# Perceiver block on one core: attention scores in 32 by 32 tiles of the array over four PSUM banks, the q projection and the scaling of probabilities at step 1

## The chip, the cores and the metric

The program runs on one core of a Trainium2 chip. The metric is the device time of one execution in microseconds; before the change three executions took 1400.08, 1402.43 and 1406.96 us (median 1402.43).

## What is computed

x is (32, 32, 512), that is 32 batches of 32 rows; ctx is (32, 257, 512). Three parts follow one another, each with a layer norm ahead and x added behind:

```python
x = x + xattn(layernorm(x), ctx, ctx, mask, Wq, bq, Wk, bk, Wv, bv, Wo, bo)   # 16 heads of 32, softmax over 257
x = x + attn(layernorm(x), Wqkv, bqkv, Wout, bout, gamma, beta)               # causal linear attention, elu + 1
x = x + ffn(layernorm(x), gate_w, shared_*, expert_*)                         # 64 experts, top 8 by sigmoid, I = 256
# in xattn, for each batch:
scores = einsum('bnlh,bnph->bnlp', q, k) / sqrt(32)   # 16 heads, 32 x 257 each
out    = einsum('bnlp,bnph->bnlh', softmax(where(mask, scores, -1e8)), v) @ Wo.T + bo
```

## The kernel before

Two stages follow one another on the core. `stage_a` (lines 96 to 1018) computes both attentions, the shared part of the experts for the first four row tiles and the routing; `stage_b` (from line 1049) loads the experts' weights and computes them for gathered rows. The change touches `stage_a` alone. What follows is about it.

The 1024 rows of x make 8 tiles of 128 rows, of 4 batches each. Every engine has its own instruction queue, in which it goes through the same walk (`body`, line 206): for each tile t, for each of its batches b, six steps k = 0 to 5; the step's number in the tile is s = 6 b + k. The engines meet through semaphores. Tiles 0 and 1, the last tile and a closing pass are written out, the tiles between are a loop (`passes`, line 221). A queue is served strictly in order, so what stands ahead of an instruction on its engine holds it up even where its data are ready.

For batch n = 4 t + b, TensorE does (`per_batch`, line 833): at k = 0 to 3 one fourth of the keys each (12 matmuls, into banks 0 and 1 in turn), at k = 4 and 5 half of the values each (12 matmuls of 512 columns, banks 0 and 1). Keys and values are computed as three products of rounded parts (`ch` high, `cl` low). The softmax of a batch is finished while the next one is projected ("carried"): the scores of batch n are computed in steps 4 and 5, two groups of four heads each (line 891). For that ScalarE writes q of the batch into `qb`, a matrix of 128 x 128 for each group whose blocks off the diagonal are zero (`q_blocks`, line 428), so one matmul over all 128 rows gives four heads. The two score banks (2 and 3) serve the four groups in turn, and VectorE clips each by the mask into `prob` (line 638), then takes the maximum (641) and the bias of the exponential (643). ScalarE exponentiates two groups at step 0 and two at step 1 of the next batch (`exps`, line 443); VectorE scales by the reciprocal of the sum at step 2 (`scaled`, lines 586 to 595). At step 4 TensorE transposes the probabilities in two halves through one bank (`prob_t`, line 827; the bank is `at_ps`, number 4) which ScalarE copies to `att` (line 472), and at step 5 multiplies them by the values into `av_ps`, bank 5 (lines 878, 879). VectorE adds the last position's value and writes `ot` (`attended`, line 597).

Two lists place other work in these steps. `PRE` prepares the next tile: the layer norm of x at step 4 ("norm": VectorE, with a root on GpSimd, line 369, for which VectorE waits), its transposes at step 18 ("xT", line 803), its q projection at step 20 ("q", `pre_q`, lines 809 and 557). `POST` (line 67) finishes the tile before: output projection at step 6 ("oproj", line 933), transposes of the normed x at 9, q, k, v of the linear attention at 10 and 11 (lines 941, 945), its products at 14 to 17 (lines 954, 964), "outproj" at 19 (line 968) whose result goes through two norms on VectorE (lines 696 to 706), the transposes of the third norm's result at 22 ("x3T", line 936) and the router (line 971) with a chain of short operations on VectorE (707 to 733), and "pos" at 23, after which VectorE computes the slot indices (744) and GpSimd scatters eight columns of entries (line 407). GpSimd's root for the next "norm" stands behind these scatters. In the closing pass the rest of the last batch and tile is done, with the shared experts between (`SHARED`, line 70).

## Time and profile before

| | us |
|---|---|
| median of three runs | 1402.43 |
| the profiled execution | 1397.42 |
| its span, first to last instruction | 1395.7 |
| TensorE busy | 1302.3 (93%) |
| VectorE busy | 780.5 (56%) |
| ScalarE busy | 628.1 (45%) |
| GpSimd busy | 395.6 (28%) |
| mean granted TensorE clock | 0.979 |

All rows come from the one profiled execution. Times are microseconds from the start of its span. PE is TensorE, DVE VectorE, ACT ScalarE, POOL GpSimd, SP SyncE; Lnnn is a line of the kernel. A matmul in float32 shows as two records. Its duration includes the way through the array, so records overlap and the distance between two starts is what each costs TensorE in a row. What stands in square brackets is the idle time of the engine just before, with what ended it.

### The profile page before, as it was taken

What the parts mean: (1) busy time and instruction counts of PE and PEld (TensorE: products, weight loads), DVE (VectorE), ACT (ScalarE), POOL (GpSimd) and SP (SyncE); (2) the same over time, 40 slices, a digit from 0 to 9 for tenths busy, and PEclk for the clock granted to TensorE, in tenths of its full rate; (3) what the DMA queues carried; (4) which work ended last, traced back from release to release, by engine and by line L of the source; (5) the groups of instructions that cost most, each with busy time, mean ns of one, the idle gap of its engine ahead of it and who ended that gap; (6) DMA issues with size and microseconds to landing.
All of it is one profiled execution on the core that took longest, in us unless ns stands there. A gap on an engine that the chain in (4) does not pass through costs nothing. (4 is left out here: it accounts for less than half of the span.)

```text
span 1395.7 us, 28249 instructions
## 1 busy us (share of the span) xinstructions
PE 1302.3 (93%) x7526; PEld 1006.9 (72%) x7527; DVE 780.5 (56%) x1758; ACT 628.1 (45%) x1312; POOL 395.6 (28%) x314
## 2 busy tenths in 40 slices
PE   5999999999999999999997878999999999999991
PEld 4888878888887878788885534676676766667660
DVE  4445665665655656656565454656655565655540
ACT  3453444353443434443432105566656565665550
POOL 0002020030020200300301113356655556856531
PEclk9999999999999999999999989999999999999996
DMA  6722110201110101101003006799999999999884
GB/s 202 285 89 44 32 48 17 63 17 40 39 32 31 47 16 46 32 16 55 25 1 121 16 32 242 247 317 327 343 300 299 270 333 311 367 291 311 261 217 84
DMA packets 67186, 204.74 MB, mean 147 GB/s; under 512 B 16047, under 2 KB 18351, under 8 KB 56768
## 3 DMA queue, kind: packets, MB, share of 16 engines
q1 hardware_dynamic: 43248, 159.71, 31.6%
q0 software_dynamic: 23888, 44.40, 15.2%
q8 instruction: 27, 0.44, 0.1%
q14 instruction: 23, 0.19, 0.0%
HBM read 177.26 MB, written 37.03 MB: 154 GB/s over the span
## 5 line engine op out<-in xcount | busy, mean ns | idle before, releaser
L369 POOL TENSOR_TENSOR rstd<-vep,half 128x1 f32<-128x1 f32 x32 | 17.8, 556 | 576.4 <-DVE vep L532 576.3
L457 ACT ACTIVATE kt<-bank,colb 128x256 f32<-128x256 f32 x128 | 60.6, 474 | 243.4 <-PE bank L848 243.4
L846 PE MATMUL bank<-ch,wkh 128*128 128x256 f32 x512 | 158.6, 310 | 7.5 <-DVE cl L543 7.5
L1490 PE MATMUL ebank<-guh,xth 128*128 128x512 f32 x380 | 155.0, 408 | 1.6 <-DVE xtl L1383 0.8
L1378 DVE TENSOR_TENSOR gul<-wgu,guh 128x2048 fp32r<-128x2048 f32 x54 | 123.8, 2293 | 54.2 <-ACT guh L1295 54.2
L1225 POOL DMA_INDIRECT xg<-xn_rows,ig x95 | 126.9, 1336 | 87.9 <-issue 72.9
L1492 PE MATMUL ebank<-guh,xtl 128*128 128x512 f32 x380 | 149.1, 392 | 0.0
L1491 PE MATMUL ebank<-gul,xth 128*128 128x512 f32 x380 | 148.3, 390 | 0.0
L848 PE MATMUL bank<-ch,wkl 128*128 128x256 f32 x512 | 144.6, 282 | 0.0
L847 PE MATMUL bank<-cl,wkh 128*128 128x256 f32 x512 | 144.5, 282 | 0.0
L1520 PE MATMUL ebank<-wd,ht 128*128 128x512 f32 x292 | 134.3, 593 | 0.8 <-ACT ht L1280 0.8
L846 PEld LDWEIGHTS bank<-ch,wkh 128*128 128x128 f32 x512 | 97.6, 191 | 16.0 <-issue 14.3
L1295 ACT CAST guh<-wgu 128x2048 fp32r<-128x2048 f32 x54 | 102.9, 1906 | 7.5 <-DMA wgu<-in_egu 7.4
L862 PE MATMUL bank<-wvh,ch 128*128 128x512 f32 x256 | 105.6, 413 | 0.0
L407 POOL DMA_INDIRECT slot_table<-entry,idx x61 | 59.9, 981 | 153.3 <-DVE idx L744 137.1
L1285 ACT ACTIVATE sg<-ebank 128x256 f32<-128x256 f32 x95 | 36.5, 385 | 145.4 <-PE ebank L1492 135.5
L847 PEld LDWEIGHTS bank<-cl,wkh 128*128 128x128 f32 x512 | 97.7, 191 | 5.3 <-issue 5.0
L864 PE MATMUL bank<-wvh,cl 128*128 128x512 f32 x256 | 101.3, 396 | 0.0
L863 PE MATMUL bank<-wvl,ch 128*128 128x512 f32 x256 | 100.9, 394 | 0.0
L848 PEld LDWEIGHTS bank<-ch,wkl 128*128 128x128 f32 x512 | 97.4, 190 | 0.0
L1373 DVE TENSOR_TENSOR h<-ebank,sg 128x256 f32<-128x256 f32 x95 | 40.0, 424 | 86.3 <-ACT sg L1285 84.9
L1520 PEld LDWEIGHTS ebank<-wd,ht 128*128 128x128 f32 x292 | 51.4, 190 | 45.2 <-issue 44.0
(244 smaller groups left out, 2774.6 us busy)
## 6 DMA issues: line engine op xcount, KB each, us to landing
wgu<-in_egu SPq DMA_DIRECT2D x54, 1024.0 KB, 8.5
wd<-in_edn SPq DMA_DIRECT2D x54, 512.0 KB, 6.2
sgu<-in_egu SPq DMA_DIRECT2D x17, 1024.0 KB
craw<-in_ctx SPq DMA_DIRECT2D x32, 514.0 KB, 3.2
sdn<-in_edn SPq DMA_DIRECT2D x17, 512.0 KB, 5.3
wqkv<-in_wqkv SPq DMA_DIRECT2D x1, 3072.0 KB, 18.5
second_sums<-x1b SPq DMA_DIRECT2D x9, 256.0 KB, 3.7
xa<-in_x SPq DMA_DIRECT2D x8, 256.0 KB, 2.8
```

Of the source, the lines that this page charges most:

```text
L846: mm(out, wkh[:, c, w], h[:, c, :], start=c == 0, stop=False)
L847: mm(out, wkh[:, c, w], lo[:, c, :], start=False, stop=False)
L848: last = mm(out, wkl[:, c, w], h[:, c, :], start=False, stop=c == DC - 1)
L862: mm(out, h[:, c, r], wvh[:, c, :], start=c == 0, stop=False)
L864: last = mm(out, lo[:, c, r], wvh[:, c, :], start=False, stop=c == DC - 1)
L1225: nc.gpsimd.indirect_dma_start(tile.xg[item.q][:, :], None, d.xn, bass.IndirectOffsetOnAxis(ig[item.q][:, tile.half:tile.half + 1], 0), bo ...
L1295: nc.scalar.copy(guh[par][:, :, :], wgu[w][:, :, :]).then_inc(s_w["gu_high"], 1)
L1378: V.tensor_tensor(gul[par][:, :, :], wgu[w][:, :, :], guh[par][:, :, :].bitcast(F32), ALU.subtract).then_inc(s_w["gu_low"], 1)
L1490: mm(out, ah[:, c, :], bh[:, c, :], start=c == 0, stop=False)
L1491: mm(out, ah[:, c, :], bl[:, c, :], start=False, stop=False)
L1492: return mm(out, al[:, c, :], bh[:, c, :], start=False, stop=c == n - 1)
L1520: last = mm(y_ps[tile.half][:, :], tile.ht[:, c, :], wd[item.w][:, c, :], start=c == 0, stop=c == IC - 1)
```

## The change

- The four heads groups' scores are computed by 16 narrow matmuls a batch: for column group g and row group i, 32 rows of `qt` by 32 columns against the same 32 rows of the keys, straight from `qt`, into rows 32 g of bank i. The zero-padded `qb`, its copies on ScalarE and its clearing on GpSimd go.
- The score banks are now four: 2, 3, 5 and 0. Bank 0 is also that of the keys' first fourth, so keys at step 0 wait for the minimum that reads it, which VectorE takes first. Transposes and attended values share bank 4.
- On TensorE the scores are all at step 5, behind the second half of the transposes, which moves there from step 4; attended values come after the scores. They read `att` with a stride, as the heads now stand in another order. The four minima are all at step 5 on VectorE, ahead of `attended`. ScalarE's copy of the second half moves to step 5, ahead of the copy of the values.
- The q projection of the next tile moves from step 20 of the tile before to step 1 of its own tile. SyncE's load of x moves from step 20 to step 18.
- Scaling moves from step 2 to step 1 on VectorE.
- On ScalarE three more tiles of the loop are written out, on VectorE one; on TensorE none.
- Buffers of the shared experts' rows that lay in `qb` become two of their own.

The diff, cut to its core:

```diff
@@ -74,7 +74,8 @@
 PER = [sum(1 for n in STEPS if BANK[n] == b) for b in (0, 1)]
-PRE = {4: "norm", 18: "xT", 20: "q"}
+PRE = {4: "norm", 18: "xT"}
+PREQ = 1
@@ -104,7 +105,7 @@
         bank = [ctx.enter_context(nc.psum_tensor(f"bank{i}", [P, 512], F32)) for i in range(8)]
-        kv_ps, sc_ps, at_ps, av_ps, px = bank[0:2], bank[2:4], bank[4], bank[5], bank[6:8]
+        kv_ps, sc_ps, at_ps, av_ps, px = bank[0:2], (bank[2], bank[3], bank[5], bank[0]), bank[4], bank[4], bank[6:8]
...
@@ -211,6 +213,8 @@
                         on_pre(PRE[s], t + 1)
+                    if front and prev and s == PREQ:
+                        on_pre("q", t)
                     if prev:
@@ -218,12 +222,15 @@
-        def passes(eng, per_batch, on_post, on_pre, on_shared=None):
+        def passes(eng, per_batch, on_post, on_pre, on_shared=None, written_out=0):
...
             body(True, True, 1, True, per_batch, on_post, on_pre)
-            with eng.Fori(2, NT - 1) as t:
+            for t in range(2, 2 + written_out):
                 body(True, True, t, True, per_batch, on_post, on_pre)
+            if 2 + written_out < NT - 1:
+                with eng.Fori(2 + written_out, NT - 1) as t:
+                    body(True, True, t, True, per_batch, on_post, on_pre)
             body(True, True, NT - 1, False, per_batch, on_post, on_pre)
@@ -285,7 +292,7 @@
             def on_pre(n, t):
-                if n == "q":
+                if n == "xT":
...
@@ -425,20 +430,9 @@
-            def q_blocks(t, b):
-
-                n = BT * t + b
-                wait(act, s_pqe, t + 1)
-                wait(act, s_sc, 4 * n - 4)
-                for i in range(HG):
-                    r = slice(i * HD, (i + 1) * HD)
-                    last = nc.scalar.copy(qb[b % 2][r, :, i * HD:(i + 1) * HD], qt[r, :, b * L:(b + 1) * L])
-                last.then_inc(s_qb, 1)
-
             act.wait_ge(s_pt, 1)
...
             high(0, 0)
-            act.wait_ge(s_pad, 4)
@@ -453,27 +447,27 @@
                     wait(act, s_kv, 6 * n + k + 1)
-                    wait(act, s_sc, 4 * n)
+                    wait(act, s_sc, n)
                     nc.scalar.activation(kt[:, k, 0:S1], kv_ps[k % 2][:, 0:S1], ACT.Identity, bias=colb[:, 1, k:k + 1]).then_inc(s_ke, 1)
...
                 if k == 3 and front:
-                    if b == 0 and type(t) is int and t == 0:
-                        q_blocks(0, 0)
-                    if b < 3:
-                        q_blocks(t, b + 1)
                     if b < 3 or nxt:
...
                 if k == 4 and carried:
-                    for j in range(2):
-                        wait(act, s_tr, 2 * (n - 1) + j + 1)
-                        nc.scalar.copy(att[:, j, :], at_ps[:, :]).then_inc(s_at, 1)
+                    attention(n, 0)
+                    if not front:
+                        attention(n, 1)
+                if k == 5 and carried and front:
+                    attention(n, 1)
                 if k == 5 and front:
                     values(n, b, k)
-                if k == 5 and front and b == 3 and nxt:
-                    q_blocks(t + 1, 0)
+
+            def attention(n, j):
+                wait(act, s_tr, 2 * (n - 1) + j + 1)
+                nc.scalar.copy(att[:, j, :], at_ps[:, :]).then_inc(s_at, 1)
@@ -512,7 +506,7 @@
-            passes(act, per_batch, on_post, on_pre, on_shared)
+            passes(act, per_batch, on_post, on_pre, on_shared, written_out=3)
@@ -615,7 +609,7 @@
                     masks(t, b + 1) if b < 3 else masks(t + 1, 0)
-                if k == 2 and carried:
+                if k == 1 and carried:
                     scaled(t, b)
@@ -627,15 +621,13 @@
                         negate_last(t, b + 2) if b < 2 else negate_last(t + 1, b - 2)
+                if k == 5 and front:
+                    wait(dve, s_tr, 2 * (n - 1))
+                    wait(dve, s_sc, n + 1)
+                    for i in (HG - 1, *range(HG - 1)):
+                        V.tensor_tensor(prob[b % 2][:, i, :], sc_ps[i][:, 0:S], cap[b % 2][:, :], ALU.min).then_inc(s_sa, 1)
                 if k == 5 and carried:
                     attended(t, b)
-                if k >= 4 and front:
-                    for g in (2 * (k - 4), 2 * (k - 4) + 1):
-
-                        wait(dve, s_sc, 4 * n + g + 1)
-                        if g == 0:
-                            wait(dve, s_tr, 2 * (n - 1))
-                        V.tensor_tensor(prob[b % 2][:, g, :], sc_ps[g % 2][:, 0:S], cap[b % 2][:, :], ALU.min).then_inc(s_sa, 1)
                 if k == 5 and front:
...
@@ -757,7 +748,7 @@
             dve.wait_ge(s_pads, 16 * (NT + 1))
-            passes(dve, per_batch, on_post, on_pre, on_shared)
+            passes(dve, per_batch, on_post, on_pre, on_shared, written_out=1)
             dve.wait_ge(s_px[0], NT * PER[0] + 1)
@@ -840,6 +831,8 @@
                     wait(pe, s_ve, 2 * n - 1 + k) if k < 2 else wait(pe, s_ke, 4 * n + k - 1)
+                    if k == 0:
+                        wait(pe, s_sa, 4 * n - 3)
                     out = kv_ps[k % 2][:, 0:S1]
@@ -865,32 +858,34 @@
                     wait(pe, s_pn, n)
+                    wait(pe, s_od, n - 1)
                     prob_t(n, b, 0)
...
                         prob_t(n, b, 1)
+                if k == 5 and carried and front:
+                    prob_t(n, b, 1)
+                if k == 5 and front:
+                    wait(pe, s_ke, 4 * n + 4)
+                    wait(pe, s_ve, 2 * n + 1)
+                    wait(pe, s_sa, 4 * n)
+                    wait(pe, s_pqe, t + 1)
+                    wait(pe, s_pte, t + 2 if b == 3 and nxt else t + 1)
+                    pe.sem_inc(tick, 1)
+                    for g in range(DC):
+                        for i in range(HG):
+                            r = slice(i * HD, (i + 1) * HD)
+                            last = mm(sc_ps[i][g * L:(g + 1) * L, 0:S], qt[r, g, b * L:(b + 1) * L], kt[r, g, :], start=True, stop=True)
+                    last.then_inc(s_sc, 1)
                 if k == 5 and carried:
...
                     wait(pe, s_ve, 2 * n)
-                    wait(pe, s_od, n - 1)
                     pb = (b - 1) % 2
...
                         w = slice(g * P, (g + 1) * P)
-                        mm(av_ps[:, w], vb[pb][:, 0, w], att[:, 0, w], start=True, stop=False)
-                        last = mm(av_ps[:, w], vb[pb][:, 1, w], att[:, 1, w], start=False, stop=True)
+                        for j in range(2):
+                            heads = att[:, j, :].rearrange("p (i g n) -> p g i n", i=HG, g=DC)[:, g]
+                            last = mm(av_ps[:, w], vb[pb][:, j, w], heads, start=j == 0, stop=j == 1)
                     last.then_inc(s_av, 1)
-                if k >= 4 and front:
-                    if k == 4:
-                        wait(pe, s_qb, n + 1)
-                    for g in (2 * (k - 4), 2 * (k - 4) + 1):
-                        wait(pe, s_ke, 4 * n + g + 1)
-                        wait(pe, s_sa, 4 * n + g - 1)
-                        if g == 0:
-                            wait(pe, s_pte, t + 2 if b == 3 and nxt else t + 1)
-                        if g == 1:
-                            wait(pe, s_pqe, t + 2 if b == 3 and nxt else t + 1)
-                        mm(sc_ps[g % 2][:, 0:S], qb[b % 2][:, g, :], kt[:, g, :], start=True, stop=True).then_inc(s_sc, 1)
-                if k == 4 and carried and front:
-                    prob_t(n, b, 1)
                 if k == 5 and b == 0 and type(t) is int and t == 0:
@@ -900,6 +895,7 @@
                 if n == "q":
+                    wait(pe, s_sa, 4 * BT * t)
                     pre_q(t)
             def on_post(n, t):
```

## Rows read from the trace of the kernel before

**Rows 1.** Busy time by stage: tile 4, expert stage; the first line names columns.
```profile
core 0: us, PE busy (x) PEld busy (x) DVE busy (x) ACT busy (x) POOL busy (x), PEclk, DMA share, GB/s
...
376.40:471.70 95.30, 92.65 (x659) 78.50 (x658) 58.25 (x141) 37.91 (x102) 12.58 (x14) 1.00 0.11 35
...
840.40:1395.70 555.30, 518.93 (x2172) 355.64 (x2172) 299.10 (x593) 317.76 (x481) 293.10 (x194) 0.97 0.92 283
```

**Rows 2.** SyncE's issues in order of time, around the end of the attention stage (start, length).
```profile
840.36 0.33 SPq L1173 DMA_DIRECT2D wgu<-in_egu  x1
```

**Rows 3.** TensorE in order of time, tile 4's fourth batch: start, length, line, operation, tiles, records.
```profile
449.01 3.60 PE L968 MATMUL bank<-wout,xt 128*128 128x512 f32 x8
...
453.86 3.73 PE L813 MATMUL bank<-xat,wq 128*128 128x128 f32 x32
...
461.65 0.60 PE L830 MATMUL bank<-cn,prob 128*128 128x128 f32 x4
462.09 1.03 PE L891 MATMUL bank<-kt,qb 128*128 128x257 f32 x4
462.98 0.66 PE L830 MATMUL bank<-cn,prob 128*128 128x128 f32 x4
463.47 0.60 PE L936 MATMUL bank<-cn,xn 128*128 128x128 f32 x4
464.88 1.10 PE L971 MATMUL bank<-gate,xt 128*128 128x64 f32 x8 [0.80 <-ACT xt L494]
```

**Rows 4.** VectorE in order of time, same batch and the next tile's first.
```profile
459.48 0.55 DVE L534 TENSOR_SCALAR xn<-x,mv,rstd 128x512 f32<-128x512 f32 x1 [0.76 <-POOL rstd L369]
...
460.19 1.14 DVE L594 TENSOR_SCALAR prob<-prob,rr 128x257 f32<-128x257 f32 x4
...
476.30 0.17 DVE L744 CAST idx<-a 128x8 int32<-128x8 f32 x1
...
488.01 1.51 DVE L534 TENSOR_SCALAR xa<-xa,mv,rstd 128x512 f32<-128x512 f32 x1 [3.25 <-POOL rstd L369]
489.44 1.18 DVE L608 TENSOR_TENSOR ot<-bank,vlc 32x128 f32<-32x128 f32 x4
490.65 0.76 DVE L638 TENSOR_TENSOR prob<-bank,cap 128x257 f32<-128x257 f32 x2
```

**Rows 5.** ScalarE in order of time, same two batches.
```profile
463.67 0.59 ACT L472 COPY att<-bank 128x512 f32<-128x512 f32 x1 [0.75 <-PE bank L830]
...
478.02 1.20 ACT L435 COPY qb<-qt 32x128 f32<-32x128 f32 x4
```

**Rows 6.** GpSimd in order of time, next tile's first batch.
```profile
487.39 0.58 POOL L369 TENSOR_TENSOR rstd<-vep,half 128x1 f32<-128x1 f32 x1
```

**Rows 7.** TensorE in order of time, end of that first batch.
```profile
487.05 1.03 PE L891 MATMUL bank<-kt,qb 128*128 128x257 f32 x4
...
490.75 3.69 PE L933 MATMUL bank<-wo,ot 128*128 128x512 f32 x8 [1.26 <-DVE ot L608]
```

**Rows 8.** TensorE in order of time, small tiles of the array in tile 4's linear attention.
```profile
429.17 1.16 PE L954 MATMUL bank<-raw,x 32*128 32x128 f32 x16
...
437.99 1.08 PE L964 MATMUL bank<-am,cn 128*32 128x128 f32 x32
```

**Rows 9.** TensorE in order of time, tile 7's fourth batch and behind it.
```profile
744.98 1.12 PE L830 MATMUL bank<-cn,prob 128*128 128x128 f32 x4 [2.88 <-DVE prob L594]
...
748.19 0.60 PE L936 MATMUL bank<-cn,xn 128*128 128x128 f32 x4
...
757.43 1.06 PE L986 MATMUL bank<-cn,craw 128*128 128x128 f32 x8 [0.90 <-DVE prob L638]
760.59 5.37 PE L995 MATMUL bank<-sgu,wq 128*128 128x512 f32 x8 [2.10 <-ACT wq L507]
```

**Rows 10.** Busy time of two stretches, same columns as group 1.
```profile
744.00:747.00 3.00, 2.02 (x7) 1.83 (x8) 0.94 (x5) 0.59 (x1) 0.00 (x0) 0.58 0.84 266
762.00:765.00 3.00, 3.00 (x5) 1.10 (x4) 1.55 (x5) 0.00 (x0) 2.39 (x3) 0.51 0.98 369
```

More of the change, by code:

```diff
@@ L133, in stage_a @@
         vlc = sb("vlc", [P, DC, NB])
-        qb = [sb(f"qb{i}", [P, DC, P]) for i in range(2)]
+        rows = [sb(f"rows{i}", [P, D]) for i in range(2)]
         prob = d.prob
@@ L162, in stage_a @@
         idx, entry = d.idx, d.entry
-        flat = [a[:, :, :].rearrange("p c s -> p (c s)") for a in (craw[0], craw[1], qb[0], qt, qb[1], xat)]
+        flat = [a[:, :, :].rearrange("p c s -> p (c s)") for a in (craw[0], craw[1], qt, xat)]
+        flat = flat[0:2] + [rows[0][:, :], flat[2], rows[1][:, :], flat[3]]
         sx, sy = [a[:, 0:D] for a in flat[:4]], [a[:, D:2 * D] for a in flat[:2]] + flat[4:]
@@ L167, in stage_a @@
         sht = [wq[:, 3, j * I:(j + 1) * I].rearrange("p (c n) -> p c n", c=IC) for j in range(2)]
-        sd_ps = [at_ps, av_ps]
+        sd_ps = [bank[4], bank[5]]
         s_sl = [sem(f"shared_rows_in{j}") for j in range(SHA)]
@@ L338, in _ @@
                 load_shared(j, sx[j], sy[j], s_sl[j])
-            sp.wait_ge(s_sc, 4 * NB)
+            sp.wait_ge(s_sc, NB)
             sp.wait_ge(s_pq, NT)
@@ L361, in _ @@
             nc.gpsimd.memset(pad[:, :, 1], 0.0).then_inc(s_pad, 1)
-            for i in range(2):
-                nc.gpsimd.memset(qb[i][:, :, :], 0.0).then_inc(s_pad, 1)
-            pool.wait_ge(s_pad, 4)
+            pool.wait_ge(s_pad, 2)
             def root(n):
@@ L649, in on_pre @@
                 if n == "q":
-                    wait(dve, s_qb, 4 * t)
                     pre_q(t)
```

2 lines of the change are left out of this document (1 added, 1 removed).

## The prediction

> **What bounds the kernel now.** I read the table of stages first. In a tile of the attention stage TensorE is busy 92.7 of 95.3 us, VectorE 58, ScalarE 38, GpSimd 13, the DMA engines 11% [rows 1]: the stage runs at TensorE's pace. The expert stage begins at 840 us with DMA at 0.92, and its first load of expert weights is issued at 840.36 [rows 1, 2], so what the attention stage saves arrives earlier one for one. Then TensorE's timeline over one tile's fourth batch [rows 3] shows where work leaves and which wait comes next; VectorE's rows [rows 4], ScalarE's [rows 5] and GpSimd's [rows 6] give the chains that run beside it; [rows 7] is the one regular wait of TensorE (1.26 us). Below, K is the start of a tile's first keys, O the end of its outproj issue. For tile 4, the next K is 471.7 (the stage table is cut there [rows 1]) and O = 449.01 + 3.03 = 452.05 (eight matmul records at 0.38).
>
> **Scores.** Now a half takes four records, 462.09 to 462.98, then the next transposes start: 0.89 us, so 1.78 a batch, 32 batches [rows 3]. After: 32 records of 257 columns, 32 rows by 32 columns of the array each. No row shows such a tile. The nearest ones: 16 records of 128 columns with 32 rows each, two row groups in turn, take 1.16 us, 0.073 a record; 32 records with 32 columns each, four column groups in turn, take 1.08 us, 0.034 [rows 8]; on the full array 32 such records take 3.73, 0.117 [rows 3]. So two and four tiles do overlap almost fully, along rows and along columns, and the four streams of the second case read all 128 rows. A record of 257 columns takes 0.22 alone. If all 16 tiles overlap, a batch is two rounds, 0.44, plus issue; if only four do, eight rounds, 1.78. Neither case of [rows 8] shows an issue limit of its own, since 0.034 is what four at a time give (0.117 / 4 = 0.029). For issue I take 0.2, for going into small tiles and back 0.25 (1.16 against 8 x 0.117 = 0.94): about 0.9. The upper bound, if 0.034 were an issue limit: 32 x 0.034 + 0.25 = 1.35.
>
> The Trainium skill (TensorE: Matmul & The Clock Gate, Part 3, measured speedup) gives 10.6 times for sixteen 32 x 32 tiles; my estimate from that page would be 16 x 0.44 / 10.6 = 0.66 us, inside the bounds above, for another data type.
>
> It hardly matters whether it is 0.7 or 0.9, because of a new order: the second transposes move from before to directly before the scores, and the attended matmuls then wait for their copy. A transpose group started at 462.98 has its copy from 463.67 to 464.26 [rows 3, 5], 1.28 after its start, 0.06 for the semaphore; it occupies TensorE 0.44, so 0.90 is left for the scores. Scores and this wait together: 0.9, a gain of 0.9 a batch. The clean-up that goes (four q copies on ScalarE, 1.20 us a batch [rows 5]) is off the path and costs or gives nothing directly; it lets the context's rounding and the xT copy come earlier. The strided read in the attended matmuls I put at nothing, as their column count stays at 128; bound 0 to 16 x 0.117 = 1.9 us a batch were it to halve the rate, for which no row speaks. Written-out loops on ScalarE and VectorE: nothing, bound plus or minus 2 us in all, since both have 40% and more idle [rows 1].
>
> **Fourth batch, O to the next K** (19.63 us). The q projection, 3.5 us, leaves it (3.73 with its tail [rows 3]), and so do the first half of the scores and the second transposes ahead of the third norm's transposes (x3T): 463.47 - 462.09 = 1.38. TensorE could then start x3T at 463.47 - 3.5 - 1.38 = 458.6. But x3T needs the norm chain on VectorE, which starts with outproj's result and ends at 459.48 + 0.55 = 460.03 [rows 4]; scaling at step 1 comes ahead of it, but its exps are over before outproj ends, so it doesn't delay it. **This is what is late next:** x3T at 460.1, a new wait of 1.5 us. From x3T to K are 8.2 us now (463.47 to 471.68); minus 0.89, plus transposes 0.44 and scores 0.9, gives 8.7. New length 8.05 + 8.7 = 16.8: gain 2.9. Had scaling stayed at step 2 the stall would be worse: its last multiply ends 1.3 us after the norm [rows 4], and the first transposes wait for it. Tile 7, which has no q projection, shows that stall: 2.88 us [rows 9].
>
> **First batch, K to oproj** (19.07). Scattering the slots holds GpSimd from the indices (476.30) to 487.39, and only then comes the root for the pre-norm; VectorE stands in its queue until the apply ends at 488.01 + 1.51 = 489.52, K + 17.8 [rows 4, 6]. The indices keep their distance from K (fewer scores, but all four minima now behind the router's chain: 0.2 earlier), so K + 17.65. Behind that apply stand the four minima (0.76 for two, so 1.52) and the addition of the values (1.18): 20.4, oproj at K + 20.5 [rows 4]. The change adds a wait here: the fourth score bank is the bank of the next keys, so keys of batch 1 wait for the first minimum, K + 18.1. TensorE comes there at 487.9 - 471.7 = 16.2 now (487.05 + 0.89 [rows 7]), plus 3.5 for q, minus 0.9: 18.8. So step 1 is where q pays: it covers this wait, with 0.7 to spare. Then keys, 20.2, and 0.3 of wait before oproj instead of 1.26 [rows 7]. K to oproj grows by 1.4. Tiles 1 and 7 have no root held up (tile 0 scatters nothing, tile 7 has no pre-norm), so there it grows by 3.5 - 0.9 = 2.6. Batches 1 and 2 lose 0.9 each. The earlier load of the next x rows on SyncE waits for the xT transposes; behind it stands one context load, landing long before its use.
>
> **Sum.** Tile 0: q 3.5 leaves it, 4 x 0.9: -7.1. Tile 1: -2.9 + 2.6 - 1.8 = -2.1. Tiles 2 to 6: 5 x (-2.9 + 1.4 - 1.8) = -16.5. Tile 7: its norm ended 1.3 before the first transposes at 744.98 (the scaling between [rows 4]), so x3T moves from 748.19 to 743.7 [rows 9], -4.5; behind it 8.2 becomes 8.7 as above, so -4.0; -4.0 + 2.6 - 1.8 = -3.2. Tail: the same order, 0. Together -28.9.
>
> **The clock.** A wait of 2.88 us was followed by a granted clock of 0.58 (most of the stretch at the 1.2 GHz level), and 0.90 idle, transposes, 2.10 idle by 0.51 [rows 9, 10], while 1.26 in every tile did not (1.00 [rows 1, 7]). The new 1.5, with short transposes and the 0.80 before the router [rows 3], lies between. A fall costs about 1.3 us of the values' matmuls; I take it in four of seven tiles: +5. Bounds 0 and +9. Total -24: from the profiled execution's 1397.4 (span 1395.7) to 1373. The median of the runs shown is 1402.4, 5.0 above it: 1378.
>
> **Rivals.** (1) Only four tiles overlap. Scores 1.78 + 0.25 = 2.03, so 1.1 x 32 = +35, of which the first batches' slack hides about 3: 1410. For it: nothing in [rows 8] goes beyond four. Against: rows and columns each give their full share. (2) Four overlap, and a weight load for a row group must wait until its running matmul is done: eight rounds of 0.22 + 0.11 (the load, put at the 0.117 pace of full records as a bound) + 0.25 = 2.9, so +2.0 x 32 = 64, less 3: 1439, slower. The whole change breaks even where scores take 0.9 + 24 / 32 + 3 / 32 = 1.75 a batch, which is 0.19 a round of eight, so both rivals are slower than before. Against: in the second case of [rows 8] all four tiles share the rows and still run at 0.034. The Trainium skill (same page, Part 3, the mechanism) says that weight loads overlap only where the row group differs, and this order returns to each row group after four matmuls; that rule speaks for (2), the trace against it. (3) The new bank wait: if the first minimum comes later than K + 18.8, each us late costs 1 us in five tiles; 3 to 4 us late adds 15 to 20: 1393 to 1398. Against: the margin is worked out, but only 0.7. (4) The change doesn't pack at all, 32 x 0.22 = 7 us a batch, 1570: the first case of [rows 8] excludes it nearly.
>
> **How the numbers follow.** Forecast 1378, chance 0.78, own range 1366 (no fall of the clock, -28.9, and some 7 us for the rest) to 1392 (scores at 1.35, +14). Rival 3: 0.06. Rival 1: 0.10. Rivals 2 and 4: 0.06. Range 1366 to 1397. A difference under 0.5% (7 us) can't be told from none. Faster by more: 0.78 + 0.03 = 0.81. Within: 0.03 and half of rival 1, 0.08. Slower: the other half and rivals 2 and 4, 0.11.
>
> **What would show it.** Scores: 32 records in 0.6 to 1.0 us a batch, attended matmuls waiting for ScalarE's copy. x3T waiting 1.3 to 1.7 us for VectorE's norm in each tile; K to K 92 in tiles 2 to 6; oproj's wait 0.6; q behind the second keys. Granted clock below 1.00 in some tiles. Wrong, if the scores take over 1.4 us, if keys wait for a minimum in the first batch, or if the expert stage doesn't move.

## The result and the profile after

| | before | after |
|---|---|---|
| median of four executions, us | 1404.70 | 1388.03 |
| lowest, highest | 1400.08, 1407.38 | 1386.48, 1388.64 |
| profiled execution, its span | 1397.42, 1395.7 | 1388.28, 1386.5 |
| mean granted clock of TensorE | 0.979 | 0.973 |
| records of TensorE's matmuls, of ScalarE | 7526, 1312 | 8294, 1184 |

The ratio after to before is 0.9883, 95% interval 0.9851 to 0.9915: faster by 1.2%. 1378 was forecast, with a range of 1366 to 1397. The medians differ by 16.7 us, the two profiled executions by 9.1, as the one of before ran below its four others; the lengths below are those of the profiles and account for the 9.1.

Busy time by stage, columns as in [rows 1]: tile 4, the closing pass and the rest of the changed kernel. The last two are cut at the start of TensorE's last group of down-projections of the shared experts, 821.6 us (828.5 in before). In this document that point is called the last K, and the time from it to the end the expert stage. The first matmul of `stage_b`, at which [rows 1] cut, comes later: at 840.4 in before and 832.2 in after, with 555.3 and 554.3 us to the end.

```profile
core 0: us, PE busy (x) PEld busy (x) DVE busy (x) ACT busy (x) POOL busy (x), PEclk, DMA share, GB/s
...
367.60:463.80 96.20, 90.91 (x755) 75.42 (x754) 58.18 (x141) 33.37 (x86) 12.72 (x14) 0.98 0.11 34
746.80:821.60 74.80, 56.17 (x295) 34.03 (x293) 35.60 (x76) 10.65 (x27) 11.94 (x13) 0.88 0.13 46
821.60:1386.00 564.40, 523.06 (x2183) 357.64 (x2182) 306.15 (x621) 317.83 (x481) 302.39 (x199) 0.97 0.91 280
```

TensorE gave back 1.7 us of busy time in tile 4, 92.65 to 90.91, and the tile still takes 96.2 us instead of 95.3 [rows 1]: its idle time doubled, from 2.65 to 5.29. Counted from one first key to the next, and from tile 7 on to the last K, the attention stage ends 6.9 us earlier and the expert stage is 2.3 us shorter, together 9.2 between the two spans. It splits so: tiles 0 and 1 -9.4 (forecast -9.2), tiles 2 to 6 +2.1 (forecast -16.5 before the clock), tile 7 -3.4 (forecast -3.2), closing pass +3.7 (forecast 0), expert stage -2.3, of which 1.2 lie ahead of the first matmul of `stage_b`. So what failed lies in tiles 2 to 6 and behind tile 7. The closing pass has two longer waits of TensorE: 3.25 us instead of 2.10 before the first of the shared experts' products, in e1 below too, and 3.37 instead of 1.37 for VectorE's addition to the last attended values, whose signal from TensorE came 2.0 us late in the way described next.

TensorE in order of time, tile 4's fourth batch, the answer to [rows 3]:

```profile
453.10 0.60 PE L821 MATMUL bank<-cn,prob 128*128 128x128 f32 x4
455.04 0.66 PE L932 MATMUL bank<-cn,xn 128*128 128x128 f32 x4 [1.34 <-DVE xn L528]
456.45 1.10 PE L967 MATMUL bank<-gate,xt 128*128 128x64 f32 x8 [0.75 <-ACT xt L488]
...
460.24 0.60 PE L821 MATMUL bank<-cn,prob 128*128 128x128 f32 x4
460.77 0.72 PE L877 MATMUL bank<-kt,qt 32*32 32x257 f32 x32
461.51 1.72 PE L887 MATMUL bank<-att,vb 128*128 128x128 f32 x13
```

This is the forecast order, row by row. The 32 records of the scores (L877) take 0.72 us; the third norm's transposes (L932) wait 1.34 for VectorE's norm (1.5 was forecast), the router 0.75; the attended matmuls (L887) start at 461.51. The row behind them is short of three records: 16 are issued. From outproj's end to the next K are 16.75 us (forecast 16.8).

The next batch, the same engine and then ScalarE and GpSimd, the answers to [rows 5 to 7]:

```profile
478.85 0.40 PE L857 MATMUL bank<-wvh,cl 128*128 128x512 f32 x1
482.20 0.74 PE L821 MATMUL bank<-cn,prob 128*128 128x128 f32 x4 [2.96 <-ACT att L470]
```

```profile
481.07 0.59 ACT L475 COPY vb<-bank 128x512 f32<-128x512 f32 x1 [5.20 <-remote]
481.56 0.59 ACT L470 COPY att<-bank 128x512 f32<-128x512 f32 x1
```

```profile
469.51 1.14 POOL L412 DMA_INDIRECT slot_table<-entry,idx  x1 [15.10 <-DVE idx L735]
...
478.80 0.96 POOL L412 DMA_INDIRECT slot_table<-entry,idx  x1 [0.30 <-issue]
479.77 0.58 POOL L374 TENSOR_TENSOR rstd<-vep,half 128x1 f32<-128x1 f32 x1
```

This was not foreseen. TensorE ended the first half of the values at 476.00 (its last record, L857, starts at 475.61 and takes 0.39), and ScalarE's copy of it started at 481.07. "Remote" means that the profile finds no instruction that ended the wait. The trace has the change of the semaphore that this record raises at 480.98: the signal came 5 us late, while GpSimd issued its scatters (K + 5.7 to K + 16.0). Four of TensorE's signals in this batch are over 1.4 us late, the first from K + 8.0. ScalarE's copy of the first transposes stands behind it in the queue, and TensorE waits 2.96 us for that. Tiles 2 to 7 show the same wait with 2.14, 2.60, 2.73, 2.96, 1.55 and 0.82 us. Behind them the clock is low:

```profile
482.20:488.40 6.20, 6.20 (x64) 4.94 (x64) 2.57 (x8) 1.07 (x2) 0.00 (x0) 0.72 0.00 0
```

K to oproj is 22.4, 24.4, 24.6, 24.7 and 21.9 us in tiles 2 to 6, where 20.5 was forecast. No signal of TensorE is over 0.7 us late in the attention stage in the profile of before, whose scatters stand at the same distance from K.

### The profile page after: what moved, and what is told of

Same layout as the page of the kernel before. It is cut to its first block and busy times, and to the rows that moved or that the text cites. A ratio compares the mean times of both kernels' runs of the same rounds, so it can differ in the third digit from the quotient of the medians.

```text
span 1386.5 us, 29315 instructions
## 1 busy us (share of the span) xinstructions
PE 1280.7 (92%) x8294; PEld 976.9 (70%) x8295; DVE 780.5 (56%) x1758; ACT 591.8 (43%) x1184; POOL 400.0 (29%) x312
## 5 line engine op out<-in xcount | busy, mean ns | idle before, releaser
L1374 DVE TENSOR_TENSOR gul<-wgu,guh 128x2048 fp32r<-128x2048 f32 x54 | 123.8, 2293 | 55.1 <-ACT guh L1291 45.8
L1221 POOL DMA_INDIRECT xg<-xn_rows,ig x95 | 130.2, 1371 | 82.7 <-issue 69.4
L857 PE MATMUL bank<-wvh,cl 128*128 128x512 f32 x256 | 102.1, 399 | 0.0
```

The source lines that it names most:

```text
L857: last = mm(out, lo[:, c, r], wvh[:, c, :], start=False, stop=c == DC - 1)
L1221: nc.gpsimd.indirect_dma_start(tile.xg[item.q][:, :], None, d.xn, bass.IndirectOffsetOnAxis(ig[item.q][:, tile.half:tile.half + 1], 0), bo ...
L1374: V.tensor_tensor(gul[par][:, :, :], wgu[w][:, :, :], guh[par][:, :, :].bitcast(F32), ALU.subtract).then_inc(s_w["gu_low"], 1)
```

## The experiments

The twelve kernels ran on four chips: e1 to e4 on one, e5 to e8 on a second, e9 to e11 on a third, e12 on a fourth, each time beside the kernel before (medians 1397.14, 1398.80, 1399.21 and 1397.35). Times are compared within a chip, lengths within the profiles. A table of them stands at the end of this section. A "fall" is a tile of 2 to 7 in which the length from outproj's end to K is over 1 us above the shortest of the kernel; in each of them the granted clock drops below 1.00.

**e1, the changed kernel again.** No edit.

> The changed kernel once more, unaltered. In its first profile TensorE's signal that half of the values is written reached ScalarE 2.6 to 5.1 us late in the first batch of tiles 2 to 6, and the step from K (first keys of a tile) to oproj took 21.9 to 24.7 us where 20.5 was forecast. Theory A (a property of the kernel): the same here, K to oproj 22 to 25 us, time 16 to 17 us under the kernel before. Theory C (a property of that one execution): K to oproj 20 to 21 us and a time about 25 us under before.

Measured: 1371.19 (1369.35 to 1372.91), ratio 0.9818 [0.9794, 0.9842], 26 us below before. K to oproj 20.2 to 20.6, outproj's end to K 16.75 in four of six tiles (the other two are falls), K to K 91.7 to 92.2 in tiles 3 to 6. The first batch of tile 5, on ScalarE and then on TensorE and VectorE:

```profile
466.69 0.59 ACT L475 COPY vb<-bank 128x512 f32<-128x512 f32 x1 [0.80 <-PE bank L857]
```

```profile
474.84 3.69 PE L929 MATMUL bank<-wo,ot 128*128 128x512 f32 x8 [0.44 <-DVE ot L602]
```

```profile
472.20 1.41 DVE L628 TENSOR_TENSOR prob<-bank,cap 128x257 f32<-128x257 f32 x4
```

The copy that came 5.20 us late now waits 0.80. With K at 454.2, the first minimum stands at K + 18.0 (forecast 18.1), the second keys start at 472.73, K + 18.5 (forecast 18.8), oproj at K + 20.6 (forecast 20.5) after a wait of 0.44 (forecast 0.3). So the late signals don't belong to the kernel alone, and where they are absent the steps of the prediction hold.

**e2, the scatters a tile later.** GpSimd issues them at step 7 of the tile after, which in a queue that works on tile t are those of tile t - 2. In short:

```
-    if n == "pos":           scatters of tile t
+    if 6 * b + k == 7:       scatters of tile t - 2
```

> The changed kernel with GpSimd's scatters of the slots moved from the end of a tile to step 7 of the tile after, behind oproj's work on GpSimd, where it has some 50 us to spare. Theory A, that the late signals come with the scatters and strike the first batch because they run there: K to oproj falls to 19.5 to 20.5 us in all tiles (the pre-norm's root is not held up either), five tiles gain 2 to 5 us and the time is 12 to 20 us under the changed kernel, unless the late signals only move along to steps 7 to 11, in which case the waits appear there and the gain is 0 to 8 us. Theory B (late signals from the written-out loops): K to oproj still 22 to 24 us, gain under 3 us.

Measured: 1381.14 (1375.37 to 1382.52), ratio 0.9892 [0.9871, 0.9913], 10 us slower than e1, where theory A had 12 to 20 under the changed kernel. This chip shows no late signals without the edit either (e1), so e2 can't tell whether they come with the scatters. K to oproj falls only from 20.2 to 20.6 to 20.0 to 20.2: TensorE's own work has that length. From outproj's end to K it is 16.8 to 20.4. Two stretches of e2, the same place of tiles 3 and 5 (columns as above), and then the rows of tile 6:

```profile
349.00:360.00 11.00, 8.89 (x34) 7.13 (x33) 7.43 (x24) 2.64 (x6) 0.55 (x1) 0.70 0.30 99
...
537.00:548.00 11.00, 8.86 (x82) 6.82 (x81) 8.30 (x27) 3.65 (x8) 0.55 (x1) 1.00 0.29 99
```

```profile
631.14 1.26 POOL L399 TENSOR_TENSOR xr<-xr,rowb 128x512 f32<-128x512 f32 x1
631.21 1.48 DVE L531 TENSOR_SCALAR xn<-x,mv,rstd 128x512 f32<-128x512 f32 x1 [0.76 <-POOL rstd L374]
632.74 0.66 PE L935 MATMUL bank<-cn,xn 128*128 128x128 f32 x4 [2.29 <-DVE xn L531]
```

Both stretches have the same x3T wait (1.35 and 1.36), and one is followed by a granted clock of 0.70, the other by 1.00. In tiles 6 and 7 a new cost comes on top: GpSimd's addition, which stood behind the scatters, now runs beside VectorE's norm, whose last step takes 1.48 instead of 0.55 us, and the wait grows to 2.29.

**e3, no written-out tiles.** Loops on ScalarE and VectorE as on the other engines. In short:

```
-            passes(act, ..., written_out=3)
+            passes(act, ...)
-            passes(dve, ..., written_out=1)
+            passes(dve, ...)
```

> The changed kernel with no tile of ScalarE's and VectorE's loops written out. Theory A: the time is that of the changed kernel within 4 us, and the late signals stay. Theory B, that written-out code (fetched from memory) makes them: K to oproj falls to 20.5 us in tiles 2 to 6 and the time by 12 to 20 us.

Measured: 1426.04 (1425.73 to 1432.89), ratio 1.0225 [1.0192, 1.0258], 55 us slower than e1 on the same chip. The attention stage costs 3.3 of it (last K 803.6 against 800.3, with three falls instead of two); the expert stage, whose code is untouched, takes 620.4 us instead of 568.0. The page of the profile counts 82 packets of instruction fetch in the second instruction queue, after has 26. The price of the written-out loops, "nothing, bound plus or minus 2", fell here.

**e4, the kernel before with its scatters a tile later**, the edit of e2 in before.

> The kernel before with its scatters moved in the same way. There no signal was late, but VectorE stood 3.25 us behind the scatters in the pre-norm and TensorE 1.26 us before oproj in five tiles. Theory A: that wait falls to 0 to 0.3, 5 x 1 = 5 to 7 us under before. If the scatters cost TensorE more than this wait by themselves, the gain is larger; if they only move their cost, none.

Measured: 1394.47 (1390.20 to 1396.03), ratio 0.9979 [0.9963, 0.9994], 2.7 us under before where theory A had 5 to 7. K to oproj goes from 19.1 to 17.65 in four of tiles 2 to 6 (19.3 to 17.9 in tile 3), as expected of [rows 7], but tile 7 takes 96.9 us (95.2) and the closing pass 72.0 (71.1): of 1.45 us a tile little reaches the end. In tile 7 the norm's last step takes 1.48 us beside GpSimd's addition, where it took 0.55, and TensorE waits 3.85 instead of 2.88 [rows 9].

**e5, scaling back at step 2.**

```
-                if k == 1 and carried:
+                if k == 2 and carried:
                     scaled(t, b)
```

> The changed kernel with one part undone: the scaling of the probabilities goes back from step 1 to step 2 of a batch on VectorE. Theory A (the prediction's): in the fourth batch the scaling then stands behind the norm chain. In e1 the norm ended at 629.64 and the x3T transposes started at 629.70; the scaling takes 1.31 us (reciprocal to last multiply), so the first transposes of the probabilities start at about 631.0 and x3T at 631.4: O to K 16.75 + 1.75 = 18.5, and 20 where the clock falls, which a wait of over 3 us makes likely in every tile. K to K 93.7 to 95.3 in tiles 2 to 6, in all +12 to +22 us over e1's 1371: 1383 to 1393. The other three batches don't change. Theory B: the place of the scaling is worth nothing, as the x3T wait only changes its name: 1371 plus or minus 4.

Measured: 1401.49 (1397.35 to 1402.85), ratio 1.0020 [1.0002, 1.0039]: this one line undoes the whole gain (e8, on the same chip, has 0.9849). TensorE and then VectorE in tile 4's fourth batch, and the stretch behind:

```profile
459.16 1.12 PE L821 MATMUL bank<-cn,prob 128*128 128x128 f32 x4 [3.08 <-DVE prob L588]
```

```profile
457.26 0.55 DVE L528 TENSOR_SCALAR xn<-x,mv,rstd 128x512 f32<-128x512 f32 x1 [0.76 <-POOL rstd L374]
457.72 0.17 DVE L585 RECIPROCAL rr<-rs 128x4 f32<-128x4 f32 x1
457.97 1.14 DVE L588 TENSOR_SCALAR prob<-prob,rr 128x257 f32<-128x257 f32 x4
```

```profile
460.00:464.00 4.00, 3.25 (x15) 2.85 (x14) 0.88 (x4) 1.17 (x2) 0.00 (x0) 0.50 0.51 163
464.00:467.00 3.00, 3.00 (x11) 2.34 (x11) 2.52 (x9) 0.21 (x1) 0.00 (x0) 0.74 0.03 5
```

The scaling stands behind the norm, the transposes wait 3.08, as theory A said, and longer than the changed kernel's 1.34 by 1.7. But outproj's end to K is 20.1 to 22.7 us in tiles 2 to 6, not 18.5 to 20: in tile 4 the clock falls to 0.50 and is low for some 7 us. Above the 18.5 of the wait alone that is 1.6 to 4.2 us a tile. Theory A had the mechanism and too small a price for the clock.

**e6, the q projection back at step 20** (a staging tile and one ScalarE copy carry q to the next tile; those lines are left out here).

```
-PRE = {4: "norm", 18: "xT"}
-PREQ = 1
+PRE = {4: "norm", 18: "xT", 20: "q"}
```

> The changed kernel with the pre-attention q projection of the next tile back at step 20, where the kernel before has it (a staging tile and one more copy on ScalarE carry q over to the next tile, since the scores still read the old q then). Theory A (the prediction's): moving q to step 1 pays because there it lies under the wait for the first minimum. Back at step 20 it fills the x3T wait of 1.34, so O to K is 16.75 + 3.5 - 1.34 = 18.9 and no clock fall is seen there; K to oproj stays at 20.2 to 20.6 in tiles 2 to 6, because keys of the second batch now wait 2.8 to 3.3 us for the minimum behind GpSimd's scatters. K to K 94.1 against 92.0: 5 x 2.1 = +10, tile 0 +2.2, tiles 1 and 7 -1.4 and -3.5, fewer clock falls -3 to -5: 1371 + 3, between 1368 and 1378. Theory B: the first minimum does not hold TensorE; K to oproj falls to 16.8, K to K 90.4, 1371 - 17 = 1354.

**e7, the same and the scatters later.**

> As e6, and the scatters of the slots moved to step 7 of the tile after, as in e2. Theory A: now neither the x3T wait (q fills it) nor GpSimd's scatters hold TensorE: K to oproj 16.8 to 17.2, O to K 18.9, K to K 90.5 to 90.9, no clock fall in tiles 2 to 6. Against e1: tiles 2 to 6 -1.3 x 5, tile 1 -1.4, tile 7 -3.5, clock -3, tile 0 +2.2: about -12, 1359. Theory B (what e2 lost, 10 us over e1 in longer O to K, is from the late scatters and not from the clock): 1369 to 1375.

Measured: e6 1434.82 (1428.95 to 1439.29), ratio 1.0273 [1.0223, 1.0323]; e7 1413.03 (1406.89 to 1416.60), ratio 1.0103 [1.0057, 1.0148]. By the end, both theories of both kernels are wrong. By the attention stage theory A is right: outproj's end to K is 18.85 in tiles 2 to 6 of both (forecast 18.9); K to oproj 20.3 to 20.9 in e6, where the second keys now wait 2.6 to 2.7 us for the first minimum, and 16.8 to 17.0 in e7 (forecast 20.2 to 20.6, and 16.8 to 17.2); K to K 90.4 to 90.9 in e7 (94.0 to 95.4 in e6, where from oproj to outproj's end up to 56.2 us are spent instead of 54.8; why is open), and its attention stage ends at 792.9, 7.4 earlier than e1's. Tile 4 of e7, and its expert stage:

```profile
359.00:449.70 90.70, 89.20 (x754) 74.04 (x754) 58.37 (x141) 33.65 (x87) 12.45 (x14) 1.00 0.12 36
792.90:1412.00 619.10, 539.45 (x2183) 364.58 (x2183) 306.85 (x621) 316.83 (x481) 288.84 (x199) 0.93 0.85 256
```

The rest is e3 again: expert stages of 617.3 and 619.4 us, 86 and 87 fetch packets. e3 made ScalarE's program shorter, e6 and e7 made it longer by one copy and its waits.

**e8, the loops of the scores swapped**: four matmuls in turn on the same 32 rows.

```
-                    for g in range(DC):
-                        for i in range(HG):
+                    for i in range(HG):
+                        for g in range(DC):
```

> The changed kernel with the two loops of the scores swapped: four matmuls in turn on the same 32 rows of the array (four column groups), then the next rows; before, each matmul had other rows than the one ahead. Theory A (all tiles overlap, and a weight load waits for nothing of its row group): 32 records in 0.6 to 0.9 us as now (0.72), the end within 4 us of e1, 1371. Theory B (a weight load waits for the running matmul on its rows): the four of a row group follow each other, 32 x 0.22 to 0.33 us if nothing else overlaps, 7 to 10 us a batch, +200 us and more; if the row groups still overlap with each other, 8 rounds of 0.33, 2.6 us, +1.9 x 32 = 61: 1432.

Measured: 1376.30 (1374.03 to 1379.35), ratio 0.9849 [0.9813, 0.9886]. In both orders, in e1 and in e8, each of the 32 groups of 32 records starts within 0.34 us and takes 0.72. K to oproj and oproj to outproj's end are those of e1. It is 5 us above e1, on another chip and just outside theory A's 4; it has four falls, e1 two. Rival 2, a load that waits for the running matmul on its rows, is out in the order made for it.

**e9, 28 satisfied waits at the start of ScalarE's program.**

```
             act.wait_ge(s_pad, 1)
+            for _ in range(28):
+                act.wait_ge(s_pad, 1)
```

> The changed kernel, nothing taken away or moved, with 28 satisfied waits added at the very start of ScalarE's program (they become 14 instructions: its compiled program has 1705 instead of 1691, as in e6 and e7). Theory A (ScalarE's expert loop is read again from memory in each pass when it lies badly against the blocks in which instructions are fetched; in e3, e6 and e7 it lay so): the attention stage as in e1, some 1 us at most; 80 to 90 instruction packets instead of 26; the expert stage 617 to 621 us instead of 565 to 568, the end at 1371 + 51 = 1422, slower than before. Theory B (the 50 us of e3, e6 and e7 come from something else that those kernels share, VectorE's program or the time at which the experts begin): 1371 to 1376, 26 packets.

Measured: 1447.78 (1445.21 to 1454.38), ratio 1.0346 [1.0310, 1.0383]. The second instruction queue in the page of the profile (packets, MB, share; the first, q8, has the same 30 packets in both kernels), then ScalarE's group for the turned hidden rows in the expert stage (busy, mean; idle before), and one of its waits:

```profile
q14 instruction: 86, 0.70, 0.1%
```

```profile
L1278 ACT COPY ht<-ebank 128x256 f32<-128x256 f32 x95 | 33.0, 378 | 68.2 <-issue 68.2
```

```profile
992.26 0.37 ACT L1278 COPY ht<-ebank 128x256 f32<-128x256 f32 x1 [7.29 <-issue]
```

The same two of the changed kernel:

```profile
q14 instruction: 26, 0.21, 0.0%
```

```profile
L1276 ACT COPY ht<-ebank 128x256 f32<-128x256 f32 x95 | 33.0, 377 | 22.8 <-issue 22.8
```

Fourteen instructions that do nothing cost 50 us and more (56 against after's expert stage, 53 against e1's): the expert stage takes 621.4 us, ScalarE stands 68.2 us at nothing that the profile shows, where it stood 22.8, one of the waits 7.29 long, and each pass of the loop, some 60 us, brings about five new packets of instructions, while after brings none once its loop runs. VectorE's program is untouched, so theory B is out. Theory A's 1422 assumed e1's attention stage; this chip shows the late signals of the first profile (K to oproj 24.6 to 24.9), and a closing pass 7.6 us longer than e1's, so the last K is at 827.1 and not at 800.3.

**e10, e3 with 178 satisfied waits.** The edits of e3 and e9, with 178.

> e3 (the changed kernel with no written-out tiles: loops on ScalarE and VectorE as on TensorE) with 178 satisfied waits added at the start of ScalarE's program (89 instructions, 1435 instead of 1346: the same remainder by 256, 155, as the changed kernel's 1691). VectorE's program is as in e3. Theory A: the expert loop lies as in the changed kernel, 26 packets or fewer, expert stage 565 to 570, the end within 5 us of e1: 1368 to 1376. So the written-out tiles are worth nothing but the place of the expert loop. Theory B (VectorE's program, or the loops themselves, cost the time of e3): 1426, 82 packets.

Measured: 1399.25 (1395.46 to 1401.15), ratio 0.9991 [0.9977, 1.0006]. 23 packets, expert stage 567.5 us: theory A for the expert stage, theory B is out. The forecast end of 1368 to 1376 missed, again where signals are late (last K 831.8). That is 4.7 us behind e9's, with three falls instead of one, as e3 was 3.3 behind e1: whether the written-out tiles give these few us or the falls differ by chance is not settled.

**e11, e7 with ScalarE's program placed.** Against e7, in short:

```
-                    wait(act, s_sc, n)
+                    if k == 0:
+                        wait(act, s_sc, n)
-            passes(act, ..., written_out=3)
+            passes(act, ..., written_out=4)
```

> e7 (q projection at step 20, scatters a tile later) with ScalarE's program brought to a remainder of 151 by 256: three of its four waits per batch for the scores' end before the key copies are left out as the first covers them, and four tiles instead of three are written out. VectorE's program is as in e7. Theory A: attention stage as in e7 (K to K 90.4 to 90.9 in tiles 2 to 6, last K near 793), expert stage 565 to 570 instead of 619: 793 + 568 = 1361, and 1357 to 1366 in all, faster than both kernels. Theory B (VectorE's program, 1913 in e6 and e7 against 1910, is what lies badly): 1412.

Measured: 1373.59 (1369.66 to 1375.97), ratio 0.9802 [0.9778, 0.9825]: 26 packets, expert stage 571.7, last K 802.2. It lies 7.6 us above the forecast range's upper end: the last K is 9 us later than forecast and the expert stage 2 us longer. Signals are late here too, and they moved along with the scatters: in e9 and e10, on this chip, the late ones lie at K + 8 to K + 16, in e11, where the scatters run from K + 25.0 to K + 35, at K + 32.4 to K + 32.8, 3.8 to 3.9 us late. They now fall on the linear attention (oproj to outproj's end 55.7 to 56.9 instead of 54.7 to 55.1 in e7). No clock falls between outproj and K in tiles 2 to 6. It is faster than before, and its ratio of 0.9802 is below the 0.9883 of the changed kernel where that meets late signals, with intervals that don't touch; the two were not run side by side. Where no signal is late, e1 has 0.9818, and e11 wasn't run there.

**e12, the scores issued twice.**

```
-                    for g in range(DC):
-                        for i in range(HG):
+                    for g, i in [(g, i) for g in range(DC) for i in range(HG)] * 2:
```

> The changed kernel with the 16 score matmuls of a batch issued twice, 64 records instead of 32 (the second 16 write the same sums again). In e1 the 32 records take 0.72 us and the attended matmuls start right behind ScalarE's copy. Theory A (the 32 records cost 0.6 to 0.72 us, and 0.05 to 0.25 of it lies under the wait for the copy of the second transposes): a batch grows by 0.4 to 0.7 us, a tile by 1.6 to 2.8, K to K 93.6 to 94.8 where signals aren't late and the clock doesn't fall; the end 13 to 22 us above the changed kernel on the same chip. Theory B (the records' own time is not what counts, a fixed cost of going into small tiles and back of 0.25 and more carries the 0.72): under 0.4 a batch, below 13 us. Theory C (the weight loads are paid somewhere the records don't show): over 0.8 a batch, 26 us or more.

Measured: 1403.98 (1402.67 to 1405.65), ratio 1.0051 [1.0030, 1.0073]. TensorE's rows in the fourth batch of tile 5, and the start of the next tile; then the line of TensorE's instruction queue:

```profile
568.87 1.50 PE L876 MATMUL bank<-kt,qt 32*32 32x257 f32 x64
570.29 2.05 PE L886 MATMUL bank<-att,vb 128*128 128x128 f32 x16
...
574.55 0.39 PE L839 MATMUL bank<-ch,wkh 128*128 128x256 f32 x1 [1.81 <-issue]
```

```profile
q8 instruction: 70, 1.15, 0.3%
```

The second 32 records add 0.78 us (1.50 - 0.72). In tile 6, the last of the loop, the second and third batches together are 1.37 us longer than in e1 (oproj to outproj's end 56.12 instead of 54.75) and the fourth 0.69 (17.44 instead of 16.75): 0.69 a batch, theory A. So 0.1 of the 0.78 lies under the wait for ScalarE's copy. K to oproj grows by 0.46 alone (20.98 instead of 20.52), as 0.41 comes out of oproj's wait and q starts 0.2 later. The end is 33 us above e1, on another chip, where theory A had 13 to 22, and more than the doubling explains. Part of it is of the kind of e9: 70 packets of TensorE's instructions instead of 30. Its loop over tiles grew until it is fetched anew in each tile, and TensorE stands 8.2 us in all at the top of four tiles. These waits are in the table's lengths from outproj's end to K; in tiles 2, 4 and 5 the clock falls as well (granted 0.92 in the stretch).

| | last K | expert stage | K to oproj | end of outproj to K | falls | q14 |
|---|---|---|---|---|---|---|
| before | 828.5 | 567.2 | 19.1 to 19.3 | 19.6 to 19.7 | 0 | 23 |
| after | 821.6 | 564.9 | 21.9 to 24.7 | 16.8 to 18.3 | 2 | 26 |
| e1 after again | 800.3 | 568.0 | 20.2 to 20.6 | 16.8 to 18.3 | 2 | 26 |
| e2 scatters later | 808.3 | 565.0 | 20.0 to 20.2 | 16.8 to 20.4 | 4 | 26 |
| e3 loops | 803.6 | 620.4 | 20.2 to 20.5 | 16.8 to 19.7 | 3 | 82 |
| e4 before, scatters later | 824.9 | 569.4 | 17.6 to 17.9 | 19.7 to 20.4 | 0 | 23 |
| e5 scaling at 2 | 832.9 | 568.0 | 20.2 to 20.5 | 20.1 to 22.7 | – | 26 |
| e6 q at 20 | 811.8 | 617.3 | 20.3 to 20.9 | 18.8 to 18.9 | 0 | 86 |
| e7 q at 20, scatters later | 792.9 | 619.4 | 16.8 to 17.0 | 18.8 to 18.9 | 0 | 87 |
| e8 rows outer | 807.8 | 566.9 | 20.2 to 20.6 | 16.8 to 19.9 | 4 | 26 |
| e9 28 waits | 827.1 | 621.4 | 24.6 to 24.9 | 16.8 to 18.3 | 1 | 86 |
| e10 loops, 178 waits | 831.8 | 567.5 | 24.8 to 26.0 | 16.8 to 19.8 | 3 | 23 |
| e11 e7 placed | 802.2 | 571.7 | 16.8 to 17.0 | 18.8 to 18.9 | 0 | 26 |
| e12 scores twice | 835.1 | 565.6 | 20.8 to 21.0 | 17.4 to 21.4 | – | 26 |

Lengths are of tiles 2 to 6, times and lengths in us. Falls are counted in tiles 2 to 7, in before, e4, e6, e7 and e11 in tiles 2 to 6, and not in e5 and e12, whose other waits lengthen the stretch. q14: packets in the second instruction queue.

## Why the prediction was right, and where it was not

The time fell within the range, 10 us above the forecast. Where no signal is late, in e1, the changed kernel is 26 us under before, and the sum had 24: the mechanism held. Two things in it are luck. The forecast put nothing for the place of the expert loop, worth 50 us; that the changed kernel has the good one is no part of its reasoning. And the range held the cost of late signals, of which it knew nothing, because it left room for other troubles. The sum of tiles 0 and 1 (-9.4, forecast -9.2) is nearer than its parts, -6.2 and -3.2 where -7.1 and -2.1 were forecast. The way there, step by step:

- **Scores, 0.9 with the wait.** Right. All 16 tiles overlap: 32 records in 0.72. Rivals 1, 2 and 4 are out, and e8 shows that the order of the row groups doesn't matter, against the rule of the Trainium skill (TensorE: Matmul & The Clock Gate, Part 3, the mechanism) that the prediction gives for rival 2, that weight loads overlap running matmuls only where the row group differs. Doubled, a set costs 0.78 on the engine, 0.69 a batch (e12). The issue limit of 0.034 a record that the upper bound of 1.35 allowed is not there: 32 records start within 0.34 us.
- **x3T becomes late, 1.5 us.** Right: 1.34 to 1.38 in tiles 2 to 6, 1.2 to 1.3 in tiles 1 and 7. End of outproj to K 16.75, forecast 16.8. That scaling at step 1 is what keeps it so short is shown by e5: 3.08 of wait and 30 us over e1.
- **K to oproj 20.5, with 0.7 us to spare for the first minimum.** Right by e1: minimum at K + 18.0, keys at K + 18.5, oproj at K + 20.6. Wrong in the profile of after, 22 to 24.7: the forecast has no term for signals that come late. This is the step that failed, and it is where rival 3 put its mechanism, though in another shape: not the minimum but ScalarE's queue. It accounts for tiles 2 to 6: their first batches are 15.5 us longer than forecast, 12.0 of it in the waits named above and the rest mostly at the low clock behind them; two falls between outproj and K add 3. e9 and e10, on a third chip, show it too; e1 to e8 and e12 do not. What makes one chip, or one occasion, show it stays open. That it goes with the scatters is shown by e11, where the late signals moved with them on the chip of e9 and e10; no run on that chip was without scatters, and the way in which a scatter holds up a signal isn't shown. Whether the kernel before meets them there isn't known, as it has no profile from that chip; its time there, 1399.21, is within 2.1 us of the others. A second term is wrong in the closing pass, "the same order, 0": the wait before the shared products grew by 1.15 us.
- **Strided read in the attended matmuls, nothing.** Right: 16 records in 2.05 us, 0.117 from start to start.
- **Clock, four falls at 1.3 each, +5.** The count was near: two to four in tiles 2 to 7 of after, e1, e2, e3, e8 and e10, one in e9. The price was too small: a fall lengthens the stretch between outproj and K by 1.5 to 3.4 us (the two of after by 3.1 in all). With an x3T wait of 1.2 to 1.5 us (2.2 and 2.3 in e2's last two tiles) the clock falls in 19 of 42 tiles (after, e1, e2, e3, e8, e9, e10); where q fills the wait (e6, e7, e11, tiles 2 to 6), in none of 15, and in their tile 7, which has no q projection to fill it, the length is 18.1 to 19.1 again, against 16.5. The Trainium skill (TensorE: Matmul & The Clock Gate, Part 1) has the clock set by how busy TensorE has recently been. The traces agree in direction; but equal waits with both outcomes (0.70 and 1.00 behind 1.35 in e2) show that the length of the one wait does not decide it alone.
- **Moving q to step 1.** The reason given, that q covers the wait for the first minimum, is right: with q gone K to oproj is unchanged (e6, 20.3 to 20.9), and the second keys wait 2.6 to 2.7 us for the minimum. As a choice it is second best: with the scatters a tile later, q at step 20 makes a tile of 90.7 (e7), against 91.6 in e2's tiles without a fall and 92.0 in e1.
- **Written-out loops, 0 plus or minus 2.** Wrong in the mechanism. That ScalarE and VectorE are idle 40% of the time says nothing on it. The tiles written out move the expert loop, 800 us later, to another place in ScalarE's program, and the place is worth 50 us. That the changed kernel has the good place gave the forecast its right sign; with plain loops the same change would have been slower than before (e3, 1.0225). e10 shows that the expert stage needs nothing else of them: with plain loops and the good place it takes 567.5 us. What they give the attention stage is 5 us or less and not told from the falls.

## What to carry to other kernels

Price an edit also by what it does to the place of every later loop in its engine's program. Look at the instruction queue in the profile and at an engine's idle time that nothing releases; if both jump, move the loop by a few instructions before judging the edit. When a wait remains on TensorE, fill it with work that can stand elsewhere too, as q here: that took the wait and the fall of the clock behind it. The cost of a kernel's waits beside the scatters changed here from chip to chip, so compare on more than one.

## What the runs showed of the hardware

- **A loop that is fetched again in each pass.** ScalarE's compiled program has 1691 and 1435 instructions in after and e10, a remainder of 155 by 256, and a remainder of 151 in e11; these run the expert loop without new fetches. It has 1346 in e3 and 1705 in e6, e7 and e9, remainders of 66 and 169; these fetch about five packets of 8192 bytes in each pass. The code from the start of the loop on is the same in all, so the loop's place follows from these numbers. The Trainium skill (Advanced Engine Details and Errata, ISA Cache) gives two blocks of 256 instructions for an engine and four times as much for TensorE. The runs fit that: a shift of 14 instructions decides whether the loop is fetched again in each pass, and a shift by 256 more or less changes nothing. That the loop touches a third block in the bad places is inferred, as its own start and length were not read. TensorE's loop over tiles is fetched again in each tile in e12, with 128 more matmul records and as many weight loads a tile, at 8.2 us in four tiles.
- **Late signals.** In the profile of after and on one of the four chips of the experiments, TensorE's semaphores changed up to 5.1 us late while GpSimd's scatters ran, and moved with them (e11); it cost TensorE 1.6 to 3.1 us in each of tiles 2 to 6 of after, e9 and e10.
- **GpSimd beside VectorE.** A norm's last step of 512 columns takes 0.55 us alone and 1.48 beside a GpSimd addition of 1.26 (e2, e4).
- **Small tiles.** Sixteen float32 matmuls with 32 rows, 32 columns and 257 columns of data occupy TensorE 0.72 to 0.78 us, in either order of rows and columns. As full-array matmuls of the kernel before, the same scores took 1.78.
